# Who copies the turned probabilities of the small attention units, VectorE behind its maximum or ScalarE in front of its exponential

## The reference

```python
# block 1: attention over channels (8 heads of 24 channels), with residual
q, k = l2norm(q), l2norm(k); attn = softmax(einsum(q, k) * temperature)   # 24 x 24 per head
x = x + w_proj @ (attn @ v) + b_proj
# block 2: on tokens t (1024 x 192)
att = softmax(where(causal, q @ k.T / sqrt(192), -inf))    # 6 heads of 32 channels, 1024 x 1024
t = t + att @ v                                            # input layer-normed
h = gelu(bitlinear(layernorm(t), W1, b1)); t = t + bitlinear(h, W2, b2)
```

## Time and profile before

| | |
|---|---|
| median of three runs | 4620.59 us |
| the profiled execution, its own time | 4622.14 us |
| its span (first to last instruction) | 4620.3 us |
| TensorE busy (matmuls) | 4051.6 us, 88% |
| VectorE busy | 3328.1 us, 72% |
| ScalarE busy | 2688.6 us, 58% |
| GpSimd busy | 363.2 us, 8% |
| mean granted TensorE clock | 0.976 |

### The profile page before, as it was taken

One profiled execution on the slowest core, in us unless ns is written; L12 is line 12 of the kernel. 1 busy time (PEld: TensorE's weight loads), 2 busy tenths in 40 slices (PEclk: granted clock), 3 DMA queues, 4 the chain that ended last, 5 costly groups with the idle time before them and its releaser, 6 DMA issues.

```text
span 4620.3 us, 114708 instructions
## 1 busy us (share of the span) xinstructions
PE 4051.6 (88%) x39240; PEld 2942.2 (64%) x39240; DVE 3328.1 (72%) x6327; ACT 2688.6 (58%) x5901; POOL 363.2 (8%) x374
## 2 busy tenths in 40 slices
PE   6989988979999888999888879999888999888888
PEld 4667665566766646667665666666646666665665
DVE  5777776767777767777776767777767777776776
ACT  2555556556656655565566556665655555556555
POOL 1000002000000110000002000000110000002000
PEclk7999999999999999999999999999999999999999
DMA  2111111011221101111111011211101111111011
GB/s 71 36 36 36 43 36 28 0 49 36 49 50 36 36 0 42 36 36 36 42 36 28 0 49 42 55 39 36 36 0 42 36 36 42 36 36 28 0 42 42
DMA packets 48635, 160.95 MB, mean 35 GB/s; under 512 B 12420, under 2 KB 12934, under 8 KB 48006
## 3 DMA queue, kind: packets, MB, share of 16 engines
q1 hardware_dynamic: 48134, 154.39, 14.0%
HBM read 28.52 MB, written 25.17 MB: 12 GB/s over the span
## 4 chain that ended last, share of the span: by engine, by line
PE 61%; DVE 16%; issue 15%; ACT 4%; POOL 2%; DVEq 1%; DMA 1%; ACTq 0%; SPq 0%; POOLq 0%
PE PT L686 10%; PE OUT L706 10%; PE S L672 5%; PE PT L804 5%; PE S L731 4%; DVE nmax L1206 4%; DVE work L378 4%; PE S L630 2%; PE FR L630 2%; PE S L775 2%; PE FR L574 2%; DVE XT L1077 2%; PE FR L637 1%; PE S L637 1%; PE S L674 1%
## 5 line engine op out<-in xcount | busy, mean ns | idle before, releaser
L929 ACT ACTIVATE work<-S,nmax 128x256 f32<-128x256 f32 (+7 forms) x1536 | 1137.2, 741 | 1115.0 <-DVE nmax L1206 1056.0
L1206 DVE TENSOR_REDUCE nmax<-S 128x1 f32<-128x256 f32 (+7 forms) x1536 | 1156.0, 753 | 780.2 <-PE S L674 760.4
L686 PE MATMUL PT<-ident,work 128*128 128x128 f32 x6912 | 1111.5, 281 | 224.8 <-DVE work L378 195.6
L686 PEld LDWEIGHTS PT<-ident,work 128*128 128x128 f32 x6912 | 746.7, 142 | 441.4 <-DVE work L378 259.4
L378 DVE COPY work<-PT 128x512 f32<-128x512 f32 (+3 forms) x1536 | 892.8, 581 | 41.4 <-PE PT L686 35.3
L672 PE MATMUL S<-KS,QS 128*128 128x512 f16 (+3 forms) x1152 | 323.6, 336 | 62.2 <-ACT work L929 29.0
L674 PE MATMUL S<-causal,identb 128*128 128x128 bf16 x1536 | 339.4, 221 | 0.0
L672 PE MATMUL S<-odd 128*128 128x512 f16 (+3 forms) x1152 | 314.8, 328 | 22.9 <-ACT work L929 21.5
L933 ACT ACTIVATE work<-PT 128x512 f32<-128x512 f32 (+3 forms) x768 | 330.6, 430 | 3.5 <-PE PT L686 3.4
L1240 DVE TENSOR_REDUCE gm<-S 128x1024 f32 (+1 forms) x180 | 220.0, 1222 | 119.4 <-PE S L775 119.1
L706 PE MATMUL OUT<-work,odd 128*32 128x128 f32 x6912 | 304.9, 277 | 0.0
(11 more groups left out here) (207 smaller groups left out, 5952.6 us busy)
## 6 DMA issues: line engine op xcount, KB each, us to landing
X<-in_x SPq DMA_DIRECT2D x32, 768.0 KB, 5.3
odd<-hi_z SPq DMA_DIRECT2D x128, 192.0 KB, 4.2
odd<-odd SPq DMA_DIRECT2D x128, 192.0 KB, 4.2
out_y<-work SPq DMA_DIRECT2D x64, 384.0 KB, 3.8
QS<-hi_z SPq DMA_DIRECT2D x64, 192.0 KB, 4.0
QS<-odd SPq DMA_DIRECT2D x64, 192.0 KB, 4.0
KS<-hi_z SPq DMA_DIRECT2D x64, 192.0 KB, 4.3
KS<-odd SPq DMA_DIRECT2D x64, 192.0 KB, 4.6
```

Of the source, the lines that this page charges most:

```text
L686: last = tr(bank[:, P * (j - c0):P * (j - c0) + P], PS[m % 2][:, m // 2 % 2, P * j:P * j + P], ident[:, :])
L929: A(PS[n % 2][:, n // 2 % 2, 0:w], S[:, n % 2, 0:w], ACT.Exp, bias=nmax[:, n % MAXES:n % MAXES + 1], accum_out=rowsum[:, sum_col(n):sum_co ...
L1206: v.tensor_reduce(nmax[:, n % MAXES:n % MAXES + 1], S[:, n % 2, 0:P * (qtile(n) + 1)], AX.X, ALU.max, negate=True).then_inc(max_made, 1)
```

## The change

`by_act` now gives ScalarE the S-chunk too. ScalarE issues that copy in front of the exponential of the slot, and the copy of L1 stays behind it. VectorE keeps L0 alone. `chunk[2]` is the unit's number.

```diff
         def by_act(i, chunk):
 
-            return chunk[1] == "p" and chunk[3] > 0
+            return chunk[1] == "p" and (chunk[3] > 0 or small(chunk))
+
+        def small(chunk):
+
+            return chunk[2] % 2 == 0
 ...
                         A(oT[:, :], OUT[0:CH, :], ACT.Copy).then_inc(oT_made, 1)
+                    for i, c in chunks_at(images, n):
+                        if by_act(i, c) and small(c):
+                            pt_copy(act, lambda o, x: A(o, x, ACT.Copy), g, images, i)
                     if n < UNITS * images:
 ...
                     for i, c in chunks_at(images, n):
-                        if by_act(i, c):
+                        if by_act(i, c) and not small(c):
                             pt_copy(act, lambda o, x: A(o, x, ACT.Copy), g, images, i)
```

## The result

The changed kernel took 4539.81 us (four runs, 4538.63 to 4540.19) against 4617.10 (four runs, 4612.91 to 4620.93). The ratio is 0.983, with a 95% interval of 0.9816 to 0.9845: 77 us less. The forecast was 4524 us, 97 under the 4620.59 known then, so the time is 16 us above it; the other 4 us between 97 and 77 are the kernel before, whose median came out lower with a fourth run. The profiled execution took 4540.2 us.

What follows compares the result with a forecast made beforehand. TensorE was taken as the bound, with 9.7 us idle in a 105.5 us image. Gains at seven places summed to 3.11 us an image, 99.5 over 32, less about 3 for first images: 4524 us, 8-in-10 range 4462 to 4578.

Steps and rivals of the forecast that it cites:

- C: Slot 8: L0 and L1 come earlier because VectorE no longer does a 256-column S-chunk copy first; 0.33 us an image.
- E: Slots 25 to 31, VectorE full with layer norm: 0.80 us by relief, plus 0.15 for L0 in slot 32; 0.95.
- D: Slots 13 to 18: L1 0.5 us earlier, then 0.2 from a copy leaving VectorE's channel-softmax chain; 0.70.
- G: Slots 46 and 47: VectorE reaches L0 earlier by a copy of 384 columns; 0.27 us an image.
- walk: Place-by-place sum of gains through one image, 3.11 us; chance 72%, own range 4495 to 4555 us.
- A: Slot 2: L1 follows L0 without a wait, as idle ScalarE copies the S-chunk in time; 0.59 us an image.
- B: Slot 4: L1's longest wait, 1.05 us, only becomes a wait of the scores for an exponential; gain 0.
- F: Slots 34 and 35: some two thirds of L1's 0.39 us wait is won before ScalarE holds TensorE; 0.27.
- third rival: ScalarE reaches the copy late, so L1's bank is no earlier and the exponential is delayed; 4704 us, chance 5%.

Runs made afterwards that it cites:

- dve_front: Kernel before the change, with VectorE keeping the S-chunk copies but doing them in front of its maximum: 4777.26 us, ratio 1.035.
- behind: Changed kernel, with ScalarE copying the S-chunks behind the slot's exponential instead of in front of it: 4949.36 us, ratio 1.071.
- ballast: Changed kernel, plus an unneeded VectorE maximum over constants, as wide as the S-chunk, at each old copy place: 4641.3 us, ratio 1.0059.
- e_only: Kernel before the change, with only the S-chunks of units 22, 24, 26 and 28 moved to ScalarE: 4609.6 us, ratio 0.9979.

## Why the prediction was right, and where it was not

**The bound and the exchange.** TensorE's waits for S-chunk copies were the thing to win; dve_front and behind show that without an early bank, bought with idle time of ScalarE, nothing is won. The load on VectorE counts too, and for more: ballast, with the load back, lost C, most of E, the second part of D and G in its timeline, 1.65 of 2.74 us. Both parts of the walk hold.

**A, B, C and D** came out to 0.02 us each. B was the test of the idea that a wait is worth only the room to the next gate: the longest wait of all gave nothing.

**E** was sized at 0.95 and is 0.81. Of the 0.80 over ScalarE's chain 0.74 had arrived by slot 30, and of the 0.15 for L0 in slot 32 there came 0.07. **G** was sized at 0.27 and is 0.39, all of it relief of VectorE, as it was 0 in ballast.

**F** is the term that failed, 0.27 forecast and -0.07 measured. The prediction took the exponential at 2106.59 as one that had waited 0.56 us for its maximum, so that the copy would just fit. In ordinary images it does not. ScalarE before the change, with PEld's wait at L1 as the last row:

```profile
1999.01 0.81 ACT L882 ACTIVATE zt<-S 128x768 f16<-128x768 f16 x1
...
1999.70 0.91 ACT L929 ACTIVATE work<-S,nmax 128x768 f32<-128x768 f32 x1
...
2000.31 0.20 PEld L686 LDWEIGHTS PT<-ident,work 128*128 128x128 f32 x2 [0.31 <-DVE work L378]
```

And after:

```profile
1965.18 0.81 ACT L886 ACTIVATE zt<-S 128x768 f16<-128x768 f16 x1
...
1965.87 0.61 ACT L928 ACTIVATE work<-PT 128x512 f32<-128x512 f32 x1
...
1966.35 0.92 ACT L936 ACTIVATE work<-S,nmax 128x768 f32<-128x768 f32 x1
...
1967.41 0.11 PEld L676 LDWEIGHTS S<-odd 128*128 128x128 f16 x2 [0.28 <-ACT work L936]
```

Before, the exponential already followed the front's copy (L882) without idle: ScalarE was full. After, the S-chunk's copy pushes it back by 0.48, and the scores of slot 35 wait 0.28 for it. The image that I had read was not an ordinary one. Two windows of the kernel before, both from slot 31 on, ahead of the place, in the ordinary image and in the one that I had read:

```profile
1993.20:1997.00 3.80, 2.86 (x24) 2.04 (x25) 3.31 (x7) 3.51 (x8) 1.47 (x1) 1.00 0.01 2
2098.80:2104.00 5.20, 4.35 (x25) 3.46 (x25) 4.36 (x9) 3.77 (x8) 1.38 (x1) 0.67 0.01 3
```

At 2098.80 to 2104.00 the clock was 0.67, so TensorE came late and ScalarE seemed to have room. That image ran to 2138.0, not 2136.6; by accident my cut of it had the length of an ordinary one. The third rival was right at F, for this slot alone.

**The images at the ends.** The gain of each image of the profiled executions, from its first scores to those of the next (us; the last image to its slot 47):

| group | first image | four in the middle | last image |
|---|---|---|---|
| 1 | 0.98 | 13.88 | 1.90 |
| 2 | 0.71 | 9.19 | 1.85 |
| 3 | 0.76 | 10.66 | 1.86 |
| 4 | 1.85 | 12.32 | 0.17 |
| 5 | 2.40 | 13.90 | 1.84 |
| the last two images | 0.80 | | 1.08 |

I took off 3 us for the first images. In fact they won 7.5 us in all, where six times 3.11 less 3 is 15.7. A and C gave next to nothing there, the last stretch of two images lost 0.9 us at its slot 2, and in four of the five groups the clock fell behind slot 31 where it had not before, at 1.4 us each. The last image of each group, where ScalarE does a layer norm, four steps in slot 37 and four in slot 38, has one wait that the change made; a weight load in slot 40:

```profile
2398.38 0.31 PEld L690 LDWEIGHTS PT<-ident,work 128*128 128x128 f32 x3 [2.60 <-ACT work L928]
```

L1 waits 2.6 us for an S-chunk copy that stands behind the norm, in five images (11.8 us in the waits above), and the scores behind it come 0.9 later than they otherwise would. That is the third rival's mechanism, where it is not covered.

**The sum.** The two profiled executions are 81.9 us apart (4622.1 and 4540.2), where the walk had 97. The first images make 8 of the missing 15 us. Each of the 20 images in the middle is 0.37 under the forecast at full clock, 7.4 us in all, but the clock gave 5 of these back: its stretches had cost these images 12 us before (by the excess over an ordinary image) and cost them 6.6 after. The last images, with what lies outside the images, won 14.5 where six times 3.11 is 18.7. It is luck that the clock hardly entered the total: over all images the stretches cost about 14 us before and 14 after (an estimate from the same excess), in other places. Waits for copies were forecast at 50 and are 54.5, and 11.8 for the new copies; those for the exponential at 110 and are 144.9, since F and the last images add to them.

Not settled: why A and C gave nothing in the first images, and what decides in which image the clock falls.

## What to carry to other kernels

Price a wait by the room up to the next thing on that engine that would not be ready, not by its own length: seven places added up to within 0.4 us of 2.7 that way, and the longest wait was worth nothing. Ask for each place whether it pays by the earlier buffer or by the relief of the engine; here the relief was the larger part, but paid only with the early buffer. A copy moves well to an engine that idles in front of an instruction which waits anyway, and only in front of it; count the slots in which that idle time is not there. Before walking one period of a repeating program, check that its granted clock is that of its neighbours, and its length too.

## What the runs showed of the hardware that I had not expected

- The granted clock answers to small changes of the schedule. Kernels with the same work but for the engine and place of the small copies had mean clocks from 0.955 to 0.978. A stretch at the lower level came behind a wait of 1.4 us of TensorE in slot 18 in some images and not in others with the same timeline up to there; five unused matmuls in the wait removed all of these. Put into the changed kernel, they made the stretches come up elsewhere, and 1.5 us were won.
- Such a stretch made one image of e_only 1.5 us longer, twice what its edit gained in an image. In ballast the runs ordered themselves by it: 4628 us at 0.967, 4640 and 4642 at 0.963, 4656 at 0.960.
- The same copy of 512 columns takes ScalarE less time than VectorE, and a little more in front of an exponential than behind one. By shape, of the changed kernel (total us, mean ns of one, idle before):

```profile
L928 ACT ACTIVATE work<-PT 128x512 f32<-128x512 f32 x192 | 116.7, 608 | 47.2 <-PE PT L690 46.6
L940 ACT ACTIVATE work<-PT 128x512 f32<-128x512 f32 x192 | 113.0, 588 | 0.0
```

VectorE's took 682 ns, in the groups of the page above.
